# LoRA merges of the second FFN's down-projection blocks by one VectorE operation each

## The reference

```python
x = x + attn_ref(cond_ref(x, itok_B_0_7, W, Wr, A, B), up_w, gate_w, ..., ffn_gate_w, ffn_up_w, ffn_down_w)
x = x + ffn_ref(cond2_ref(x, itok_B_0_23, W, b, lora_As, lora_Bs), w1, w3, w2, A1, B1, A3, B3, A2, B2)
```

```python
def lora_linear(x, w, a, b):                  # SCALING = 2.0, rank 16
    return x @ w.T + ((x @ a.T) @ b.T) * SCALING
g = silu(lora_linear(x, w1, A1, B1)) * lora_linear(x, w3, A3, B3)
out = lora_linear(g, w2, A2, B2)
```

## Time and profile before

| What | Value |
|---|---|
| median of 3 runs | 439.17 us (439.08 to 439.51) |
| the profiled execution | 439.03 us |
| its span | 437.3 us |
| TensorE matmul busy | 432.4 us (99%) |
| VectorE busy | 355.7 us (81%) |
| ScalarE busy | 248.8 us (57%) |
| GpSimd busy | 41.4 us (9%) |
| granted TensorE clock | 1.0 (2.4 GHz) over the span |

### The profile page before, as it was taken

One profiled execution on the slowest core, in us unless ns is written; L12 is line 12 of the kernel. 1 busy time (PEld: TensorE's weight loads), 2 busy tenths in 40 slices (PEclk: granted clock), 3 DMA queues, 4 the chain that ended last, 5 costly groups with the idle time before them and its releaser, 6 DMA issues.

```text
span 437.3 us, 5678 instructions
## 1 busy us (share of the span) xinstructions
PE 432.4 (99%) x1957; PEld 355.3 (81%) x1957; DVE 355.7 (81%) x537; ACT 248.8 (57%) x371; POOL 41.4 (9%) x65
## 2 busy tenths in 40 slices
PE   8999999999999999999999999999999999999996
PEld 6788888888888888888888888888888888888875
DVE  4756699676888867987799589799988799988787
ACT  6455443427566446664574658586754566755660
POOL 1003200000000010003400000010001010001000
PEclk9999999999999999999999999999999999999999
DMA  8506800044555655665551024054646454433305
GB/s 274 169 0 181 223 1 1 9 122 104 130 130 129 171 134 125 132 153 144 157 169 49 18 67 97 0 121 100 144 92 137 118 102 112 96 97 99 70 2 192
DMA packets 22317, 47.79 MB, mean 109 GB/s; under 512 B 2897, under 2 KB 4961, under 8 KB 22289
## 3 DMA queue, kind: packets, MB, share of 16 engines
q1 hardware_dynamic: 16992, 32.51, 24.4%
q0 software_dynamic: 5296, 14.92, 18.5%
HBM read 37.98 MB, written 2.10 MB: 92 GB/s over the span
## 4 chain that ended last, share of the span: by engine, by line
PE 97%; DVE 2%; issue 1%; DVEq 0%
PE PS L1612 21%; PE PS L1613 20%; PE PS L1614 20%; PE PS L1458 9%; PE PS L1459 9%; PE PS L1460 9%; PE PS L1771 1%; PE PS L1525 1%; PE PS L1682 1%; PE PS L1684 1%; PE PS L1683 1%; PE PS L1466 1%; PE PS L1465 1%; PE PS L1464 1%; DVE WU L913 0%
## 5 line engine op out<-in xcount | busy, mean ns | idle before, releaser
L1612 PE MATMUL PS<-HT,WU 128*128 128x512 f32 x294 | 114.9, 391 | 0.0
L1613 PE MATMUL PS<-HT,WU 128*128 128x512 f32 x294 | 114.6, 390 | 0.0
L1614 PE MATMUL PS<-HT,WU 128*128 128x512 f32 x294 | 114.4, 389 | 0.0
L544 ACT ACTIVATE WU<-raw 128x256 fp32r<-128x256 f32 (+2 forms) x62 | 58.3, 940 | 31.2 <-PE PS L1614 16.2
L913 DVE TENSOR_TENSOR WU<-raw,WU 128x256 fp32r<-128x256 f32 (+2 forms) x63 | 67.1, 1065 | 4.8 <-ACT WU L544 4.7
L544 ACT ACTIVATE PS<-PS 128x512 f32<-128x512 f32 x62 | 36.2, 584 | 60.4 <-PE PS L1614 39.7
L544 ACT ACTIVATE G<-T 128x512 fp32r<-128x512 f32 (+3 forms) x62 | 51.0, 830 | 27.8 <-DVE T L1154 14.8
L1612 PEld LDWEIGHTS PS<-HT,WU 128*128 128x128 f32 x294 | 55.2, 188 | 12.4 <-DVE PS L1116 0.9
L913 DVE TENSOR_TENSOR G<-T,G 128x512 fp32r<-128x512 f32 (+3 forms) x59 | 55.0, 941 | 12.2 <-ACT G L544 11.6
L1614 PEld LDWEIGHTS PS<-HT,WU 128*128 128x128 f32 x294 | 55.2, 188 | 11.7
L1613 PEld LDWEIGHTS PS<-HT,WU 128*128 128x128 f32 x294 | 55.2, 188 | 10.9
(11 more groups left out here) (186 smaller groups left out, 696.2 us busy)
## 6 DMA issues: line engine op xcount, KB each, us to landing
raw<-in_pieces SPq DMA_DIRECT2D x73, 256.0 KB, 3.0
raw<-in_parts SPq DMA_DIRECT2D x14, 512.0 KB, 3.8
raw<-delta POOLq DMA_DIRECT2D x14, 512.0 KB, 5.6
raw<-in_parts POOLq DMA_DIRECT2D x14, 384.0 KB, 5.1
X<-in_x SPq DMA_DIRECT2D x8, 256.0 KB, 5.4
raw<-in_pieces SPq DMA_DIRECT2D x14, 128.0 KB, 3.5
out_x<-X SPq DMA_DIRECT2D x7, 256.0 KB, 2.1
su_raw<-in_stk_up POOLq DMA_DIRECT2D x6, 192.0 KB, 5.9
```

Source lines behind the costliest of these rows:

```text
L544: return nc.scalar.activation(o, i, ACT.Copy)
L1612: pe.matmul(bank, w[:, 1, cols], hi, start=start and kc == 0, stop=False, skip_group_check=not start)
L1613: pe.matmul(bank, w[:, 0, cols], low, start=False, stop=False, skip_group_check=not start)
L1614: mm = pe.matmul(bank, w[:, 0, cols], hi, start=False, stop=kc == 1, skip_group_check=not start)
```

## The change

`MERGED` now also names all blocks of the second FFN that are not up blocks: 19, 20, 25, 26 and 29. For these five, `delta_hi` on ScalarE and `merge_by_dma` on GpSimd's queue are left out, and VectorE calls `merge_block(q + 2)` in `steady(q)`, q = 17, 18, 23, 24 and 27, between `add_b(q)` and what follows. The waits of `part1_hi`, `sums` and `banks_free` go to the semaphore `merged` for them, and `merged_by_dma` counts only the nine blocks left. `sums` keeps its wait for the low part two blocks before for all blocks from 16 on.

```diff
-MERGED = {("block", F2): 1, ("block", F2 + 1): 2, ("piece", 0): 3}
+MERGED = {_what: _n + 1 for _n, _what in enumerate(
+    [("block", _q) for _q in range(F2, END + 1) if _q < F2 + 2 or BLOCKS[_q][1] != "u"] + [("piece", 0)])}
...
         def merged_by_dma(q):
-            return q - F2 - 1
+            return sum(("block", p) not in MERGED for p in range(F2, q + 1))
...
             for q in range(F2 + 2, END + 1):
                 if q in (F2 + 5, F2 + 9, F2 + 11):
                     su_load({F2 + 5: 3, F2 + 9: 4, F2 + 11: 5}[q])
-                merge_by_dma(q)
+                if ("block", q) not in MERGED:
+                    merge_by_dma(q)
...
-                elif q < F2 + 2:
+                elif ("block", q) in MERGED:
                     act.wait_ge(merged, MERGED["block", q])
...
                 copy_bc(q)
-                if F2 < q <= END - 2:
+                if F2 < q <= END - 2 and ("block", q + 2) not in MERGED:
                     delta_hi(q + 2)
...
-                if q < F2 + 2:
+                if ("block", q) in MERGED:
                     dve.wait_ge(merged, MERGED["block", q])
                 else:
                     dve.wait_ge(merged_in, 16 * merged_by_dma(q))
+                if q > F2 + 1:
                     dve.wait_ge(w_ready, P_TWO[q - 2] + 1)
...
                 add_b(q)
+                if F2 + 1 < q + 1 < END and ("block", q + 2) in MERGED:
+                    merge_block(q + 2)
                 if odd:
                     b2_lo(s, c)
                 add_d(q)
```

## The result

The changed kernel takes **441.40 us** (median of 4 runs, 440.96 to 441.57) against 439.12 (median of 4, 438.85 to 439.51): ratio 1.0050, 95% interval 1.0039 to 1.0062. It is slower by 2.3 us; 441.15 was forecast. The profiled execution took 440.96 us, 1.93 more than that of before, for which the forecast's sum was 1.98.

A forecast was written before the change was run, and what follows sets the result against it. TensorE, busy 99% of the span, was taken to bound the kernel. Two full pairs at 0.99 us gave 1.98; added to 439.03 that is 441.0, plus 0.14 for the median: 441.15 us, range 440.1 to 442.2.

The forecast's parts named there:

- Where: Distance between merge matmuls grows by about 0.5 us in each of blocks 17, 18, 23, 24 and nowhere else.
- Length of the operation: Each new VectorE merge pushes its follower by 1.14 us, with 1.25 as the upper bound.
- Rival 2: Each new operation holds VectorE its full length, 1.25 for 1.14 in four merges: 0.44 us more, 441.6; chance 0.12.
- Gain of 0.08 us at `t1_lo`: In steady(17), without ScalarE's copy ahead, VectorE's `t1_lo` starts 0.08 us sooner.
- Block 17 late by 0.54, pair late by 0.99: VectorE's delay less TensorE's slack of 0.52: 1.06 gives 0.54 us at block 18's start, 1.51 gives 0.99 after the pair.
- the three absorbed waits: In block 18 VectorE makes up 0.69 us in existing waits for ScalarE's SiLU, TensorE and ScalarE's copy.
- Block 27 at nothing: The 1.14 us merge fits in VectorE's 1.27 us idle before `add_d(27)`: cost 0, up to 1.14 without that cover.
- Rival 1: Not slower: ScalarE's copy and the DMA held VectorE up; two 0.3 us gaps vanish, 438.6; chance 0.10.
- Rival 3: VectorE's merge waits for block 20's second weight load if it exceeds 5.9 us: 445.0; chance 0.06.
- The signs: New waits of p4 and p6 (lines 1612, 1682) for VectorE's `add_d` and low part, about 2 us in total.
- The sum: Two full pairs at 0.99 us each: 1.98 us slower in total.
- TensorE makes nothing up: In blocks 19 to 22 TensorE cannot recover lateness, as its stream had no gaps.

The follow-up runs named there:

- only_29: Kernel before with only block 29's merge moved to VectorE; 19, 20, 25 and 26 stay with ScalarE and the DMA: 439.36 us against 439.22.
- removed_alone: Changed kernel with the five VectorE operations merging only 4 of 1024 columns, copies and DMAs gone: 439.48 us, kernel before 438.98.
- changed_reordered: Changed kernel, merges of 19, 20, 25, 26 later, copy_e, add_b and block 29's low part earlier, merge matmuls of 21, 27 after p5: 439.06 us (before 438.98).
- late_place: Changed kernel with merges of 19 and 25 after the next block's low part, 20 and 26 between t4_sum and t4_lo: 439.73 us, kernel before 439.22.

## Why the prediction was right, step by step

- **Where**: only blocks 17, 18, 23 and 24 grow, 27 does not. Right in the stage table and in only_29.
- **Length of the operation**: 1.14 taken, 1.13 measured (306.03 to 307.16; 315.36 to 316.49). Rival 2's 1.25 is refuted; the 1.25 us behind a merge of before is not the operation's own. The Trainium skill (VectorE: DVE Perf Modes, "The DRAIN you can't avoid") states that the next operation does not start until the pipe is empty, and ends by pointing to an exception for one that is not held. Here the follower begins 0.08 us before the shown end of the merge, so the trace goes with the exception, which its section "Two Vector instructions with no wait between them" describes: an instruction is held back when it starts in another group of 32 partitions than those before it, as the follower in the earlier trace rows does.
- **Gain of 0.08 us at `t1_lo`**: `t1_lo` follows 0.34 us behind `part1_lo` (303.95 to 304.29), as against 0.42. Right.
- **Block 17 late by 0.54, pair late by 0.99**: the stages grew by 0.49, and by 0.93 and 1.05 per pair. The merge of block 20 was forecast for 315.43 and began at 315.36; the three absorbed waits went as written. The restart behind VectorE is there too: p6(18) begins at 309.56, 0.06 us behind the low part.
- **Block 27 at nothing**: in the changed kernel `add_d(27)` begins 1.36 us after the merge where 1.13 is back to back, so 0.23 us of waiting for TensorE are left, and the stage stays 10.03. Right. (The 1.27 us of the earlier trace rows count from the shown end of the instruction ahead; from where `add_d` could have begun it was 0.09 more.) VectorE in that place:

```profile
406.36 1.22 DVE L1284 SCALAR_TENSOR_TENSOR raw<-PS,raw 128x1024 f32<-128x1024 f32 x1
407.72 0.69 DVE L1125 TENSOR_TENSOR T<-PS,T 128x512 f32<-128x512 f32 x1
```

- **Rival 1** (ScalarE and the DMA held VectorE up) fell: removed_alone keeps the three waits on `add_b`, and gives -0.22 us of stretch, not -0.6. Its price was set too high: the 0.3 us per gap are idle notes of weight loads, and TensorE's stages lose 0.22 and 0.18 (10.25 and 10.21 against 10.03), so it should have read -0.4, which stands closer to what was measured. **Rival 3** (the load not there) fell too: VectorE shows no idle time ahead of either merge in the rows above.
- **The signs**: the new waits of p4 and p6 are there, all at line 1619 (1612 before); line 1689 (1682 before), which was named too, belongs to block 29, and its wait is unchanged at 0.8 us. The new ones add up to 3.3 us in the view, not to about 2, as these are idle notes of weight loads again.
- **The sum**: 1.98 forecast, 1.93 between the profiled executions, 2.3 between the medians. The difference of 0.3 is within the interval (1.7 to 2.7 us) and has no place in the trace. That the sum comes within 0.05 of the profiled pair is in part luck: its own pairs are 0.93 and 1.05.
- **TensorE makes nothing up**: from the merge matmuls in block 19 to those in block 23 it took 40.14 us before (320.59 to 360.73) and takes 40.10 in the changed kernel (321.51 to 361.61), with the lateness of a whole pair behind it.

What is not shown: why block 23 grew by 0.61 us and block 17 by 0.49. VectorE's low part begins 7.52 us behind the first merge matmul there and 7.45 in block 17, and block 23 was 0.04 us shorter before; what makes VectorE those 0.07 us later is open.

## What to carry to other kernels

Where one engine's stream has no gaps, the price of an operation moved to another engine is not its length but what is left of it after the slack ahead of the next result that the full engine waits for: beside the kernel before, half the length cost 0, the whole cost 2 us, the whole elsewhere in the queue 0.4. Find that slack (end of the result, start of its reader) before moving anything, and put work behind the results that are waited for, not ahead; then look at which buffer the later place gives back later. The waits that the queue's own order makes are the first thing to take: two reorderings brought 0.9 us, while taking five DMAs and five copies away brought 0.2 in the stretch and nothing that the medians can tell.

## What the runs showed that was not expected

The time until the second FFN varies by about 1 us between executions of kernels that do the same there: TensorE's merge matmuls of block 14 began at 250.02 us in only_29 and at 251.22 in changed_reordered, and the waits for the first low parts of x (three loads of weights near 9 us) were 0.9 us in all in the kernel before, and 2.0 in late_place, whose own twelve runs reach from 439.31 to 441.25. What makes the first low parts late is not shown. The waits of late_place's weight loads there:

```profile
PEld PS L1487 <- DVE HT L917: 2.0, 3, 0.9
```

A difference of some tenths between two profiled executions is therefore read from the edited stages alone.
